# The last output rows of a sparse transformer layer: the second batch's chunks taken in another order

## The reference, cut to what matters

```python
k = int(CAP * s); kc = k - 1                      # 512, 511
sel_idx = jnp.sort(topi[:, :kc], axis=1)
x_sel = x[bidx, sel_idx]
...                                               # attention of the selected tokens
x1 = x_sel + o
x2 = x1 + jax.nn.gelu(rmsnorm(x1, ln2) @ w1) @ w2
proc = x2 * w_sel[..., None]
out = jnp.zeros_like(x).at[bidx, sel_idx].set(proc)
return out + x * (1.0 - sel_mask)[..., None]
...
x = _layernorm(x + _L0_ffn_ref(x, ...), axis=-1)
```

## Time and profile before

| what | value |
|---|---|
| time, median of 3 runs | 489.78 us (489.71, 489.78, 492.18) |
| profiled execution, its own time | 493.17 us |
| its span, first to last instruction | 491.0 us |
| busy share: PE, DVE, ACT, POOL | 91%, 81%, 59%, 37% |
| mean granted clock of TensorE | 0.976 |

### The profile page before, as it was taken

How to read it: one execution, slowest core, us unless ns; L and a number is a source line. 1 busy time by engine, 2 the same in 40 slices (tenths; PEclk the granted TensorE clock), 3 DMA queues, 4 the chain that set the end, 5 groups by cost and what they waited for, 6 DMA issues and landing times. The chain is left out here.

```text
span 491.0 us, 10264 instructions
## 1 busy us (share of the span) xinstructions
PE 445.9 (91%) x3525; PEld 331.1 (67%) x3525; DVE 396.8 (81%) x1227; ACT 287.6 (59%) x616; POOL 183.8 (37%) x231
## 2 busy tenths in 40 slices
PE   8798999999999987999898999998998999998960
PEld 5587888777777733677675666676885666675860
DVE  4778898789888899869598999979768999976740
ACT  3436555554455435036569999956347999973700
POOL 9356667766777650265361000002006000001641
PEclk9899999999999999999998999999999999998995
DMA  7713342244221211056950000000000000000110
GB/s 241 245 44 89 124 133 87 85 129 130 87 86 55 75 45 44 21 202 219 334 170 2 1 3 1 2 3 0 1 1 1 3 2 1 3 2 0 35 41 11
DMA packets 29370, 33.89 MB, mean 69 GB/s; under 512 B 5860, under 2 KB 24968, under 8 KB 29320
## 3 DMA queue, kind: packets, MB, share of 16 engines
q1 hardware_dynamic: 23088, 24.78, 15.6%
q0 software_dynamic: 3520, 8.40, 5.5%
q10 hardware_dynamic: 2712, 0.06, 0.3%
HBM read 19.59 MB, written 13.63 MB: 68 GB/s over the span
## 5 line engine op out<-in xcount | busy, mean ns | idle before, releaser
L1335 ACT ACTIVATE arena<-arena,nmax 128x511 f32<-128x511 f32 x128 | 91.6, 719 | 3.3 <-DVE nmax L1811 3.0
L1811 DVE CUSTOM_DVE_ANT_0 arena<-ps,nmask 128x511 f32<-128x511 f32 x128 | 84.9, 683 | 0.3 <-issue 0.3
L1005 PE MATMUL ps<-ident,arena 128*128 128x128 f32 x512 | 79.8, 279 | 4.1 <-ACT arena L1335 1.9
L1005 PEld LDWEIGHTS ps<-ident,arena 128*128 128x128 f32 x512 | 60.0, 142 | 26.0 <-ACT arena L1335 14.6
L730 PE MATMUL ps<-wgd_hi,x_hi 128*128 128x512 f32 x128 | 51.9, 405 | 0.0
L732 PE MATMUL ps<-wgd_hi,x_lo 128*128 128x512 f32 x128 | 50.5, 395 | 0.0
L731 PE MATMUL ps<-wgd_lo,x_hi 128*128 128x512 f32 x128 | 50.4, 394 | 0.0
L989 PE MATMUL ps<-arena 96*128 96x512 bf16 x128 | 48.9, 388 | 1.3 <-DVE x_sel L1876 0.5
L421 DVE COPY big<-ps 128x512 f32<-128x512 f32 x64 | 44.1, 688 | 6.3 <-PE ps L1005 5.0
L518 POOL TENSOR_TENSOR arena<-arena 128x512 f32<-128x512 f32 x30 | 38.9, 1295 | 9.8 <-DVE arena L1455 8.0
L421 ACT COPY big<-ps 128x512 f32<-128x512 f32 x64 | 37.0, 578 | 8.5 <-PE ps L1020 6.6
(11 more groups left out here) (265 smaller groups left out, 1036.7 us busy)
## 6 DMA issues: line engine op xcount, KB each, us to landing
arena<-in_L_attn_x SPq DMA_DIRECT2D x16, 512.0 KB, 4.6
out<-ob_sb SPq DMA_DIRECT2D x16, 512.0 KB, 3.2
w_sb<-in_L_ffn_w SPq DMA_DIRECT2D x2, 1024.0 KB, 11.0
mt_scratch<-nmask SPq DMA_DIRECT2D x8, 256.0 KB, 6.4
mt_scratch<-big SPq DMA_DIRECT2D x8, 256.0 KB, 3.3
big<-in_L_attn_Wg SPq DMA_DIRECT2D x1, 256.0 KB, 4.4
big<-in_L_attn_WD SPq DMA_DIRECT2D x1, 256.0 KB, 4.6
wqk<-in_L_ffn_wq SPq DMA_DIRECT2D x1, 256.0 KB, 8.2
```

Of the source, the lines that this page charges most:

```text
L1005: mm = pe.transpose(ps[:, 2 + u % 2, k * P:(k + 1) * P], pr[u % 4][:, k * P:(k + 1) * P], ident[:, :])
L1335: act.activation(pr[u % 4][:, 0:K - 1], sm[u % 4][:, 0:K - 1], ACT.Exp, bias=nmax[:, c, h:h + 1], scale=-1.0, accum_out=rsum[:, c, h:h + 1 ...
L1811: dve.tensor_tensor_reduce(sm[u % 4][:, 0:K - 1], ps[:, S_BANKS[b][u % AHEAD], 0:K - 1], nmask[b][:, c, 0:K - 1], 1.0, 3.4e38, ALU.add, AL ...
```

## The change

`PARTS` now cuts batch 1 into a part of chunk 3 alone, then a part of chunks 0 and 1, then a part of chunk 2. A new tuple, `ORDER`, lists the chunks of each batch in that order: (0, 1, 2, 3) for batch 0 and (3, 0, 1, 2) for batch 1. TensorE's loop over the second products follows it, and the two waits that counted chunks (`w2_done` on VectorE, `fin_ready` on GpSimd) count by the chunk's place in it. TensorE's wait for the split weights (`ffn_w_ready`) stands ahead of the loop instead of at its first chunk. That is the same place in its stream.

```diff
-PARTS = ((range(C),), (range(2), range(2, 3), range(3, C)))
+PARTS = ((range(C),), ((C - 1,), (0, 1), (2,)))
+ORDER = tuple(tuple(c for part in parts for c in part) for parts in PARTS)
...
-                        pool.wait_ge(fin_ready[b], c + 1)
+                        pool.wait_ge(fin_ready[b], ORDER[b].index(c) + 1)
...
-                for c in range(C):
+                if b == B - 1:
+                    pe.wait_ge(ffn_w_ready, KD + 2 * FB)
+                for c in ORDER[b]:
...
-                        if c == 0:
-                            pe.wait_ge(ffn_w_ready, KD + 2 * FB)
...
-                        dve.wait_ge(w2_done, b * C + c + 1)
+                        dve.wait_ge(w2_done, b * C + ORDER[b].index(c) + 1)
```

## The result

The changed kernel took 483.21 us, the median of 4 runs (482.76 to 483.52). The kernel before, over the 4 runs taken with it and earlier, had a median of 490.5 us (489.71 to 492.18). The ratio is 0.985 (95% interval 0.982 to 0.988), so the change saves some 7.3 us; the interval allows 6 to 9.

A forecast was written before the change was run, and what follows sets the result against it. One DMA engine moving the last, 127-row scatter was taken to bound the end. Issuing it first costs 0.42 us and saves 8.3 us of landing: 7.9 us off 489.78 gives 481.9 us, range 481.2 to 482.8, up to 484.6 with queueing.

The forecast's parts named there:

- a queue that cost nothing here: Rival: scatters behind chunk 3's, or chunk 3's behind batch 0's, are delayed; priced at 484.5 us, chance 0.12.
- the share of 0.06: DMA share while only a chunk 3 scatter runs, read as one engine of sixteen moving its 127 rows.
- The rival of the place: Rival: a batch's last scatter is slow whatever its rows, so chunk 2 would be slow: 490.2 us, chance 0.03.
- 0.37 at 131 GB/s: DMA share and rate read from the profile before as those while a 128-row scatter runs.
- the sum: Chain to the last landing: 0.42 us later issue, 8.3 us shorter landing, 7.9 us less in all.
- 1.5 us of cover: Time GpSimd would be free after chunk 3's long issue before the variance of chunks 0 and 1 is ready.
- The price of the order: Last scatter, now chunk 2's, issued 0.42 us later because the pair's two issues stand late in the chain.
- The unknown: 128-row scatters issued while a 127-row one is under way, which the trace did not show; taken as no cost.
- 3.5 us for the range: Upper allowance for stretched GpSimd issues behind chunk 3's scatter: 1.17 us for each of three.
- GpSimd was not held: Denies the slower rival, GpSimd kept by chunk 3's scatter until it lands: 493.2 us, chance 0.03.
- the ring order: Engines take descriptors in order, so three scatters' rows queue 0.9 us on the busy engine, ending 480.9, before 481.52.
- the check that I proposed: Sign of being right: a scatter issued near 469.2 takes about 10.8 us to land and 2.6 us to issue.

The follow-up runs named there:

- old_order_128: Kernel before, order unchanged, but batch 1's chunk 3 scatter writes 128 rows instead of 127: median 481.31 us, ratio 0.981 to the kernel before.
- single_parts_again: Repeat of the changed kernel with chunks 3, 0, 1, 2 of batch 1 each a part of its own, 127 rows: ratio 0.982 to the kernel before.
- new_order_128: Changed kernel, but batch 1's chunk 3 scatter, now first, writes 128 rows instead of 127: 482.03 us, ratio 0.981 to the kernel before.

## Why the prediction was right

The forecast was 481.9 us and the median is 483.21. That is above the forecast's own range, 481.2 to 482.8, and inside the wider one up to 484.6, which was kept for a queue that cost nothing here. The mechanism was right; that the time still fell into the range is owed to that allowance and not to its reason. Laid beside the changed kernel's trace, in us from the first take-up:

| step | predicted | measured |
|---|---|---|
| issue of chunk 3 | 2.78 | 467.12 - 464.34 = 2.78 |
| GpSimd held by it | 2.58 to 3.10 | 2.58 |
| chunk 1 taken up | 5.66 | 470.01 - 464.34 = 5.67 |
| issues of chunks 0 and 1 | 8.97 and 10.33 | 8.97 and 10.32 |
| issue of chunk 2 | 12.63 | 476.98 - 464.34 = 12.64 |
| its landing | 2.5 later | 2.5 later |
| end of the span | 16.7 | 16.66 |

**The cause.** That 127 rows put the transfer on one engine, read from the share of 0.06, is shown: the count alone moves the end (old_order_128), 126 is fast, 113 is slow, and the last place has no part in it. The packets of 126 rows fit 14 engines, those of 127 and 113 rows fit one. The rival of the place fell. Two readings beside it were off. The last 8 us of the kernel before are not one engine's work throughout: until about 484.3 small packets run beside the data, and the engine is alone for the 5 us behind them. For the same reason the other fifteen engines are not idle all the time that such a scatter is under way; in the changed kernel 496 small packets start between 470 and 473 us, ahead of the pair's first issue at 473.31, so it cost nothing. And 0.37 at 131 GB/s is the mean of 2 us with pauses in them, not what a 128-row scatter reaches: 477.40 to 478.00 of single_parts_again has 0.63 and 230 GB/s.

**The hiding.** The issue of chunk 3 cost nothing on GpSimd: the sum had 1.5 us of cover at the least, and GpSimd idled 2.16 us. new_order_128 shows the whole effect of the slow scatter in the changed kernel to be nil, to 0.1 us. The price of the order was 0.42 us in the sum and 0.50 between the two kernels with 128 rows.

**The unknown.** I took nothing for scatters issued behind a 127-row one, and kept 3.5 us for the range. Their issues took 1.04, 0.97 and 1.03 us: no stretching, and GpSimd was not held. Nor did the scatter of chunk 3 wait for batch 0's, which was under way until about 470: it would then have landed near 480.9, and its engine was done by 478.0. The queueing on the busy engine is real: in single_parts_again one engine works on for 0.6 us behind the others, which fits two of the shares of 0.3 us. The Trainium skill states the ring order that the prediction leans on in a passage about the queues of SyncE and ScalarE ("DMA: Bandwidth & Descriptors", section "Queues, rings and completion order"); the trace of single_parts_again agrees for GpSimd's. My estimate had that engine free 0.6 us before it mattered (480.9 against 481.52), and in the trace it was done at about 478.0, ahead of the last scatter's data at 478.4.

**The time.** The stretch shrank by 7.95 us against 7.9 in the sum. The median is 1.3 us above the forecast. Of that, 0.7 us is the kernel before, whose median rose from 489.78 to 490.5 with one more run; the other 0.6 is within what the interval of the ratio allows (6 to 9 us saved), and no run says more of it. In later timings the kernel before had a median of 491.4 and 491.6 over 17 and 11 runs, so three runs were a thin base for tenths.

What I did not foresee is the check that I proposed: "takes about 10.8 us to land" cannot be read off the landing figure once transfers overlap. It said 8.5.

## What to carry to other kernels

When the last computing instruction ends well before the span does, look at what SyncE waits for and at the DMA share in the empty stretch. A share of 1/16 is a sign that one engine is carrying the end, and hundreds of small packets for one scatter are another. The indirect scatters with a prime number of rows were slow in every order that was tried. Put such a scatter early enough that its whole landing time, not only its issue, has passed before the last one lands, or give it a row count with a large divisor, if the kernel may write the rows that this adds. Compare kernels by the stretch that the change touches, where the rest of the program varies by more than the effect that you look for.

## What the runs showed of the hardware

- A scatter of 1 KB rows took 1.0 us to issue and 2.5 to 2.6 us to land with 128 and with 126 rows, but 2.40 and 9.2 us with 113, and 2.58 to 3.10 and 10.7 to 10.8 us with 127 in the kernel before. The issue is dearer too, not only the transfer. It goes along with the number of small packets (16 and 22 against 451 and 496); that they are the reason is not shown.
- The one engine moved 21 to 27 GB/s in the stretches shown. All of them together moved 230 GB/s in 477.40 to 478.00 of single_parts_again.
- The front of the program, with the same instructions, reached the first take-up anywhere between 462.21 and 468.26 us in these profiles. The granted clock of its first 100 us was 1.00 in the three earliest (up to 463.13), 0.97 in the latest and 0.98 in the other seven. The clock is not all of it: the kernel before and the changed one had the same 0.98 there and 0.99 in 200 to 333 us, and are 2.0 us apart ahead of 333 us.
